# Running additions of softmax sums: two engines with a half each, or VectorE with both

## What is computed

```python
Q = (q @ Wq.T + bq); K = (k @ Wk.T + bk); V = (v @ Wv.T + bv)   # in 16 heads of 32
att = softmax(einsum('bhqd,bhkd->bhqk', Q, K) / sqrt(32))
out = einsum('bhqk,bhkd->bhqd', att, V) @ Wo.T + bo
x = layernorm(out + q) * gamma0 + beta0
Q_phi, K_phi = elu(x), elu(ctx)
KV = einsum('bnd,bne->bde', K_phi, ctx)
Z = 1 / (einsum('bnd,bd->bn', Q_phi, K_phi.sum(axis=1)) + 1e-6)
out = layernorm(x + einsum('bnd,bde->bne', Q_phi, KV) * Z) * gamma1 + beta1
```

## Time and profile before

| | |
|---|---|
| three runs | 1512.37, 1514.35, 1514.75 us |
| the profiled execution, span | 1509.6 us (median of the runs less span: 4.75 us) |
| TensorE busy | 1473.3 us, 98% (10584 matmuls) |
| VectorE busy | 1227.3 us, 81% (2442) |
| ScalarE busy | 900.9 us, 60% (1846) |
| GpSimd busy | 1206.0 us, 80% (1031) |
| granted TensorE clock | 9 tenths or more in all 40 slices |

### The profile page before, as it was taken

One profiled execution on the slowest core, in us unless ns is written; L12 is line 12 of the kernel. 1 busy time (PEld: TensorE's weight loads), 2 busy tenths in 40 slices (PEclk: granted clock), 3 DMA queues, 4 the chain that ended last, 5 costly groups with the idle time before them and its releaser, 6 DMA issues.

```text
span 1509.6 us, 30353 instructions
## 1 busy us (share of the span) xinstructions
PE 1473.3 (98%) x10584; PEld 1038.6 (69%) x10584; DVE 1227.3 (81%) x2442; ACT 900.9 (60%) x1846; POOL 1206.0 (80%) x1031
## 2 busy tenths in 40 slices
PE   8999999999999999999999999999999999999996
PEld 6767767676766767667677767766767767766554
DVE  6687898878788788887779788898688978899865
ACT  3464655556666666665566665665566666566664
POOL 0487787867898898877789988887789888888964
PEclk9999999999999999999999999999999999999999
DMA  7745163443425225344343425424252442520001
GB/s 222 200 144 143 54 181 128 130 128 97 122 73 157 89 90 146 105 132 138 90 129 98 135 68 158 149 87 133 79 157 77 129 127 70 148 88 26 14 23 42
DMA packets 159575, 170.14 MB, mean 113 GB/s; under 512 B 20288, under 2 KB 122048, under 8 KB 159424
## 3 DMA queue, kind: packets, MB, share of 16 engines
q1 hardware_dynamic: 157696, 167.16, 37.4%
q10 hardware_dynamic: 1728, 1.05, 0.2%
HBM read 125.97 MB, written 42.21 MB: 111 GB/s over the span
## 4 chain that ended last, share of the span: by engine, by line
PE 85%; DVE 4%; DMA 3%; issue 3%; POOL 2%; ACT 2%; SPq 1%; POOLq 0%; ACTq 0%; DVEq 0%
PE score L471 15%; PE scoreT L485 14%; PE acc L503 14%; PE misc L565 7%; PE misc L542 7%; PE misc L553 7%; PE misc L590 7%; PE misc L529 6%; PE misc L582 5%; PE acc L519 2%; DVE maxes L810 1%; POOL pair_sum L1072 1%; DMA q_stack<-q_dram 1%; PE misc L573 1%; DVE pair_sum L850 1%
## 5 line engine op out<-in xcount | busy, mean ns | idle before, releaser
L657 ACT ACTIVATE p_ring<-scoreT 128x512 f32<-128x512 f32 x1024 | 594.2, 594 | 496.9 <-PE scoreT L485 493.6
L1072 POOL TENSOR_TENSOR pair_sum<-p_ring 128x512 f32<-128x512 f32 x504 | 665.5, 1329 | 173.9 <-ACT p_ring L657 111.5
L810 DVE TENSOR_REDUCE maxes<-score 128x1 f32<-128x512 f32 x1024 | 677.3, 679 | 151.2 <-PE score L471 146.0
L471 PE MATMUL score<-k_stack,q_stack 96*128 96x512 f32 x1024 | 599.5, 587 | 5.4 <-DVE maxes L810 2.1
L485 PEld LDWEIGHTS scoreT<-q_stack,k_stack 104*128 104x128 f32 x2048 | 387.7, 191 | 156.7 <-ACT p_ring L657 81.6
L485 PE MATMUL scoreT<-q_stack,k_stack 104*128 104x256 f32 x2048 | 419.7, 287 | 7.3 <-ACT p_ring L657 5.1
L471 PEld LDWEIGHTS score<-k_stack,q_stack 96*128 96x128 f32 x1024 | 193.1, 189 | 161.5 <-issue 106.6
L503 PE MATMUL acc<-p_ring,v_sb 128*32 128x256 f32 x4096 | 249.9, 385 | 0.0
L1081 POOL TENSOR_TENSOR pair_sum<-pair_sum 128x512 f32<-128x512 f32 x189 | 248.8, 1316 | 0.0
L850 DVE TENSOR_TENSOR pair_sum<-pair_sum 128x512 f32<-128x512 f32 x189 | 197.2, 1043 | 1.9 <-POOL pair_sum L1072 1.7
L503 PEld LDWEIGHTS acc<-p_ring,v_sb 128*32 128x32 f32 x4096 | 120.6, 110 | 85.3 <-issue 3.2
(11 more groups left out here) (112 smaller groups left out, 1373.9 us busy)
## 6 DMA issues: line engine op xcount, KB each, us to landing
xT_sb<-xT_in SPq DMA_DIRECT2D x63, 512.0 KB, 3.8
q_stack<-q_dram SPq DMA_DIRECT2D x189, 128.0 KB, 2.6
k_stack<-k_dram SPq DMA_DIRECT2D x93, 256.0 KB, 4.7
ctx_nat<-ctx_in SPq DMA_DIRECT2D x32, 256.0 KB, 4.7
q_dram<-q_high SPq DMA_DIRECT2D x63, 128.0 KB, 1.9
q_dram<-q_low SPq DMA_DIRECT2D x63, 128.0 KB, 2.1
k_dram<-k_high SPq DMA_DIRECT2D x31, 256.0 KB, 2.0
k_dram<-k_low SPq DMA_DIRECT2D x31, 256.0 KB, 2.2
```

The costliest lines, as they stand in the source:

```text
L471: pe.matmul(score[k % 3][:], q_stack[0:SPLIT, unit % NQ, j, t * P:(t + 1) * P], k_stack[0:SPLIT, group_of[unit] % 2 * QUAD + j, h * HALF:( ...
L657: act.activation(p_ring[:, n % NP, h * HALF:(h + 1) * HALF], scoreT[k % 2][:], ACT.Exp, scale=SCALE).then_inc(A["exped"], 1)
L810: dve.reduce_max(maxes[:, unit % 2, t, j, h:h + 1], score[k % 3][:], AX.X).then_inc(V["maxed"], 1)
L1072: pool.tensor_tensor(pair_sum[:, place_of_pair(pair), cols], p_ring[:, (n - 1) % NP, cols], p_ring[:, n % NP, cols], ALU.add).then_inc(L[" ...
```

## The change

VectorE makes a running addition over all 1024 columns at once (`add_run` for `add_high`), and `add_low` is gone. Both halves of a pair wait for VectorE's running addition, and TensorE's ones matmul waits for one counter in place of two. In the planner's table GpSimd's 13 units for the left half go, and VectorE's addition is booked with 13 instead of 10.

```diff
@@ -256,8 +256,7 @@
             if k % 4 == 0 and k % UT > 0 and k < UT * SUMMED:
-                take("POOL", k + LEAD + 6, 13)
-                take("DVE", k + LEAD + 7, 10)
+                take("DVE", k + LEAD + 7, 13)
@@ -513,8 +512,7 @@
-                pe.wait_ge(L["run_low"], RUNS * (unit + 1))
-                pe.wait_ge(V["run_high"], RUNS * (unit + 1))
+                pe.wait_ge(V["run"], RUNS * (unit + 1))
@@ -841,13 +839,13 @@
-            def add_high(unit, p):
+            def add_run(unit, p):
 
-                whole, part = (pair_sum[:, place_of_pair(RUN_PAIRS * unit + i), HALF:2 * HALF] for i in (0, p))
+                whole, part = (pair_sum[:, place_of_pair(RUN_PAIRS * unit + i), :] for i in (0, p))
                 dve.wait_ge(L["paired"], 2 * (RUN_PAIRS * unit + p + 1))
                 if p > 1:
-                    dve.wait_ge(V["run_high"], RUNS * unit + p - 1)
-                dve.tensor_tensor(whole, whole, part, ALU.add).then_inc(V["run_high"], 1)
+                    dve.wait_ge(V["run"], RUNS * unit + p - 1)
+                dve.tensor_tensor(whole, whole, part, ALU.add).then_inc(V["run"], 1)
@@ -1065,20 +1063,10 @@
                 if p == 1 and unit > 0:
                     pool.wait_ge(T["divided"], unit)
-                elif p != 1 and pair > 0 and h == 0:
-                    pool.wait_ge(L["run_low"], RUNS * unit + max(p - 1, 0))
                 elif p != 1 and pair > 0:
-                    pool.wait_ge(V["run_high"], RUNS * unit + max(p - 1, 0))
+                    pool.wait_ge(V["run"], RUNS * unit + max(p - 1, 0))
                 pool.tensor_tensor(pair_sum[:, place_of_pair(pair), cols], p_ring[:, (n - 1) % NP, cols],
                                    p_ring[:, n % NP, cols], ALU.add).then_inc(L["paired"], 1)
-
-            def add_low(unit, p):
-
-                whole, part = (pair_sum[:, place_of_pair(RUN_PAIRS * unit + i), 0:HALF] for i in (0, p))
-                pool.wait_ge(L["paired"], 2 * (RUN_PAIRS * unit + p) + 1)
-                if p > 1:
-                    pool.wait_ge(L["run_low"], RUNS * unit + p - 1)
-                pool.tensor_tensor(whole, whole, part, ALU.add).then_inc(L["run_low"], 1)
@@ -1158,9 +1146,6 @@
                 if 0 <= pair < RUN_PAIRS * SUMMED and i < 2:
                     add_pair(pair, i)
-                unit, p = divmod(pair, RUN_PAIRS)
-                if 0 <= unit < SUMMED and p > 0 and i == 2:
-                    add_low(unit, p)
```

More of the change, by code:

```diff
@@ L159, in build @@
         V = sems("hot_rows", "phiT_low_kept", "kv_low_kept", "k_low_kept", "q_low_kept", "maxed", "max_whole", "max_high", "max_low", "max_split", "max_turned", "pad_cleared",
-                 "run_high", "den_turned", "den_inverted", "den_back", "out_scaled", "f_phi", "y_summed",
+                 "run", "den_turned", "den_inverted", "den_back", "out_scaled", "f_phi", "y_summed",
                  "mean_made0", "phi_made", "dotted", "z_added", "z_inverted",
@@ L163, in build @@
                  "centred0", "centred1", "x1_on_dve", "result_on_dve", "first_from_dve")
-        L = sems("cleared", "hot", "ident_made", "ones_made", "half_made", "paired", "run_low", "totalled", "biased", "rooted0", "eps_made",
+        L = sems("cleared", "hot", "ident_made", "ones_made", "half_made", "paired", "totalled", "biased", "rooted0", "eps_made",
                  "scaled0", "x1", "rooted1", "scaled1", "result")
@@ L1052, in vector_program @@
                 if 0 <= unit < SUMMED and p > 0 and i == 0:
-                    add_high(unit, p)
+                    add_run(unit, p)
                 unit, i = divmod(k - (VISIT_AT + 2 * VISIT + 1), UT)
```

## The result

The changed kernel takes 1517.15 us (median of 20 runs, 1513.86 to 1520.51), the kernel before 1513.24 us (20 runs, 1509.12 to 1517.77) on the same chip: ratio 1.0027, 95% interval 1.0019 to 1.0036, about 4 us slower. The forecast was 1.9 us faster. The profiled execution has a span of 1515.9 us against 1509.6, and 6.3 us is what the profiles have to explain. That is some 2 us more than the runs show: a run is 1.6 us longer than its own span (1517.5 against 1515.9 for the profiled execution of the changed kernel), so the profiled execution before, at 1509.6 in span, was 2 us faster than the median of its kernel.

A forecast was written before the change was run, and what follows sets the result against it. TensorE was taken to bound the kernel, busy 1473.3 of 1509.6 us. Terms +3.3 (middle) and −5.2 (end) make −1.9: span 1507.7, plus 4.75 to the median, 1512.4 us; range 1505 to 1520.

The forecast's parts named there:

- The order: Planner's placing of chains: some projections trade steps, TensorE's pieces stay the same; priced at nothing, bounds ±1 us.
- The prediction's sign for TensorE's chain: Test of the forecast: TensorE's chain between 115 and 1390 us would be longer by 2 to 5 us.
- The longer addition: VectorE's 189 running additions grow from 512 to 1024 columns: 1256 ns each, +109 us of VectorE time.
- The waits that go: VectorE's additions wait less for GpSimd: about 52 of 69 us go, leaving VectorE at 1284 us.
- TensorE's losses in the middle: What TensorE sees of VectorE's changed additions and waits through the score banks: +3.3 us.
- this road, through GpSimd's queue to ScalarE: Pair additions' added wait delays layer norm work queued on GpSimd, then ScalarE; 4.1 us fits in 5.3, priced at nothing.
- the 14 places: Places from 169.99 to 1423.08 us where the three score banks' slack runs out behind VectorE's addition: together 7.2 us.
- The end: From 1395 to 1447 us, where GpSimd is nearly full, dropping left-half additions gains: −5.2 us, bounds nothing and −8.7.
- The engines' part: Whole program, order priced at nothing: +3.3 us in the middle and −5.2 at the end, −1.9 us.
- The third, slower: Rival: the long addition is too much for the three score banks; 1525, half of it 1520; chance 0.25 with the fourth.
- The fourth: Rival: GpSimd spends its freed time waiting for VectorE, the end gains nothing; +3.3, 1517.7; chance 0.25 with the third.
- The distance of 4.75 us from span to median: Median of three runs, 1514.35, over the profiled span of 1509.6; kept to turn the forecast span into a time.

The follow-up runs named there:

- e2: The kernel before with only the two lines of the planner's table changed, its engines' work left as it was: 1522.3 us, ratio 1.0058.
- e3: The changed kernel with no value projection allowed within 8 steps of its weights' transfer, so one goes back to step 936: 1511.73 us, ratio 0.9988.
- e1: The changed kernel with the planner's old line for GpSimd's 13 units kept, so its order is that of the kernel before: 1514.8 us, ratio 1.0006.
- e8: The kernel before until unit 56, VectorE's long addition over both halves from unit 57 on, order of the kernel before throughout: 1509.6 us, ratio 0.9980.
- e5: The changed kernel with one value projection held back three steps, to 929, and the chains behind it moved: 1508.35 us, ratio 0.9966.
- e11: The kernel before with the changed planner's table and e5's order, engines' work as before: 1517.9 us, ratio 1.0033.
- e10: The changed kernel with the value weights of group 15 sent one step earlier, ahead of three key transfers: 1511.57 us, ratio 0.9994.

## Why the prediction was wrong

**The order, priced at nothing with bounds of ±1 us: this step failed.** Alone it costs 8.8 us (e2). With the new division it costs 1.0027 less 1.0006, about 3 us: 5.9 for V30 (changed against e3, ratios 1.0027 and 0.9988), less what the rest of the new order gives back (e3 against e1, 2.7 us, which is at the edge of the noise). I had argued that TensorE's pieces stay the same, and named only the stall of a key half behind its copy. The pieces do stay the same; the distance from a transfer to its use does not, and I had not looked at it for the value weights. The prediction's sign for TensorE's chain, 2 to 5 us longer up to 1390 us, came out at 8.3 from unit 7 to 63. The views that would have shown it are SyncE's order against TensorE's, before and after. What V30's place cost beyond the idle time, 3 us with the low clock in it, was in no term either.

**The longer addition: right.** Forecast 1256 ns, measured 1205 at the shortest and 1215 as the median. The estimate by the Trainium skill (VectorE: DVE Perf Modes, fixed extra latency), 1210 ns, was the better one.

**The waits that go: right.** Forecast VectorE 1284 us, measured 1261.1, mean of the additions 1305 ns (bound of the forecast: 1450). Over their shortest the additions lost 19 us, of 69 before; forecast were 17 left. GpSimd: 957 forecast, 962.7 measured.

**TensorE's losses in the middle, +3.3 us: the size holds, the cause only in part.** The stretches from unit 7 to 57 show +2.5 in the changed kernel, of which the order alone makes +1.2 in e2, and +4.3 in e1. One place makes over half of e1's, and it isn't a bank. Timelines of e1 on GpSimd, ScalarE, VectorE, GpSimd again and TensorE:

```profile
519.14 1.27 POOL L1069 TENSOR_TENSOR pair_sum<-p_ring 128x512 f32<-128x512 f32 x1 [2.75 <-DVE pair_sum L849]
```

```profile
525.91 0.63 ACT L712 ACTIVATE e_sb<-tiles 128x512 f32<-128x512 f32 x1 [1.04 <-POOL tiles L1095]
```

```profile
528.37 1.23 DVE L849 TENSOR_TENSOR pair_sum<-pair_sum 128x1024 f32<-128x1024 f32 x1 [0.91 <-POOL pair_sum L1069]
```

```profile
529.74 1.27 POOL L1069 TENSOR_TENSOR pair_sum<-p_ring 128x512 f32<-128x512 f32 x1 [1.40 <-DVE pair_sum L849]
```

```profile
527.08 0.50 PE L485 MATMUL scoreT<-q_stack,k_stack 104*128 104x256 f32 x2 [0.95 <-ACT p_ring L656]
528.08 0.50 PE L485 MATMUL scoreT<-q_stack,k_stack 104*128 104x256 f32 x2 [0.28 <-ACT p_ring L656]
528.52 3.32 PE L503 MATMUL acc<-p_ring,v_sb 128*32 128x256 f32 x32
```

GpSimd had waited 2.75 us for VectorE's addition and then had a scale, a bias and a shift of layer norms to do between its additions. ScalarE waits 1.04 us for that shift, and the exponential that TensorE needs is queued behind it. The prediction named this road, through GpSimd's queue to ScalarE, and put it at nothing, because a turn of 4.1 us fits into four steps of 5.3; with the layer norms' work between, it did not fit here. TensorE's two short idle times are not the whole price either: the visit behind them takes 3.32 us for the 1.93 of other visits, with the granted clock at 0.64 and then 0.50 until 532 us. So that the size holds is in good part luck; what the 14 places cost by themselves was not traced.

**The end, −5.2 us: the sign holds, the size was too large.** From unit 58 to the last transposed score e1 gains 3.8 us (in the order of before, as the term was worked out), the changed kernel 2.7; e8, where only the last units have the new division, 0.8 in its trace and 3 us by its ratio. In e5's order, without room for GpSimd's additions, the division is worth 9.5 (e11 against e5), a case that the prediction didn't have.

**Sum.** The engines' part was forecast at −1.9 us and measured at +0.9 (e1: −1.2 to +3.0). Against the measured +4.1 the miss is 6.0 us: some 3 of it are the order, the other 3, less surely, the engines' part. The time lies in the stated range of 1505 to 1520, on the other side of no change than forecast. Of the rivals none was it. The third, slower, had the banks as its cause, and e1 to e3 and e10 speak against that. The fourth has the measured time almost to the microsecond, 1517.7, and GpSimd does spend its freed time waiting; but its reason for a loss was an end that gains nothing, and the end gains 2.7 us. Its number is right by chance. The distance of 4.75 us from span to median served its end, but only 1.6 us of it lie around the program; the rest came of a fast profiled execution (2.0) and of three runs whose median lies 1.1 over that of twenty.

## What to carry to other kernels

A planner's table is part of the kernel: when a change takes a booking out, compare for each transfer the step where it is sent with the step where it is used, before and after, and give every kind of transfer a rule on that distance. Here e5, the changed kernel with one projection three steps later and eleven chains moved with it, is 0.34% faster than the kernel before (interval 0.22 to 0.46%); with the weights sent ahead of three key transfers (e10) the changed kernel is level with it. And when two engines contend, look beside their busy totals for the longest blocked operation and for what is queued behind it.

## What was not expected of the hardware

A VectorE operation with two SBUF operands was blocked not for one GpSimd addition but through seven in a row, and took 8.39 us (e11). Another, behind two, took 3.04 us. Before the change the longest running addition took 1.79 us. The Trainium skill (SBUF — State Buffer, section on who interferes with whom) has the loser blocked for the whole instruction of the other; the trace agrees for single ones (1.24 us in the prediction), and shows in addition that the blocked engine need not get its turn when that instruction ends.

After idle times of TensorE of 4.88 and 2.27 us, of 1.50 us at V30 in e11, and of 0.95 and 0.28 us a microsecond apart (e1), the granted clock was lower in the 3 to 6 us afterwards; after a single one of 0.78 us (e5) it was not. Beside the idle time itself the places of the changed kernel, e10 and e1 lost 3.0, 2.3 and 1.4 us.
